# A gated graph network: the reset gate read straight from PSUM, layer 0's product in banks of its own

## What is computed

```python
# layer 0
h = maximum(layernorm(x), 0)
x = x + (adj @ (h @ weight)) + bias
# layer 1: h = maximum(layernorm(x), 0), then five times
m  = adj @ h                       # m_in and m_out are the same product
u3 = h @ u3_w.T + u3_b
z  = sigmoid([m, m] @ w3_w.T + w3_b + u3)
r  = sigmoid([m, m] @ w4_w.T + w4_b + u3)
hv = tanh([m, m] @ w5_w.T + w5_b + (r * h) @ u5_w.T + u5_b)
h  = (1 - z) * h + z * hv
x = x + h
```

## Time and profile before

| | before |
|---|---|
| median of three runs | 1598.83 us (1595.42 to 1601.7) |
| the profiled execution's own time | 1594.64 us |
| its span, first to last instruction | 1592.9 us |
| mean granted clock of TensorE | 0.993 of full speed |
| PE busy | 1553.1 us, 98% |
| DVE, ACT, POOL busy | 67%, 50%, 22% |

### The profile page before, as it was taken

One profiled execution on the slowest core, in us unless ns is written; L12 is line 12 of the kernel. 1 busy time (PEld: TensorE's weight loads), 2 busy tenths in 40 slices (PEclk: granted clock), 3 DMA queues, 4 the chain that ended last, 5 costly groups with the idle time before them and its releaser, 6 DMA issues.

```text
span 1592.9 us, 23652 instructions
## 1 busy us (share of the span) xinstructions
PE 1553.1 (98%) x7471; PEld 721.3 (45%) x7471; DVE 1072.1 (67%) x1982; ACT 793.9 (50%) x1250; POOL 353.5 (22%) x817
## 2 busy tenths in 40 slices
PE   6999999999999999999999999999999999999997
PEld 4444444444444444444444444444444444444443
DVE  7766668666686666866677666676666766686666
ACT  3255544555445554455534555355554555454554
POOL 6230052300603006130062201430024300430000
PEclk8999999999999999999999999999999999999999
DMA  4121113211131111311122111221112211121111
GB/s 149 40 47 33 27 27 83 50 26 37 21 100 28 36 30 40 79 33 32 26 51 74 33 26 31 62 66 26 36 30 56 63 34 32 26 53 47 33 27 53
DMA packets 214238, 71.87 MB, mean 45 GB/s; under 512 B 208192, under 2 KB 209088, under 8 KB 214208
## 3 DMA queue, kind: packets, MB, share of 16 engines
q1 hardware_dynamic: 212480, 70.83, 19.2%
q10 hardware_dynamic: 1728, 0.66, 0.2%
HBM read 13.24 MB, written 8.39 MB: 14 GB/s over the span
## 4 chain that ended last, share of the span: by engine, by line
issue 51%; PE 22%; POOL 18%; DVE 6%; ACT 1%; DMA 1%; POOLq 1%; SPq 1%; DVEq 0%
PE ps_m L561 14%; POOL x_in L457 5%; POOL y L439 3%; POOL x_in L447 2%; POOL newton L330 1%; POOL newton L340 1%; PE ps_v L583 1%; PE ps_u L583 1%; PE ps_v L585 1%; PE ps_u L587 1%; PE ps_u L585 1%; PE ps_v L587 1%; POOL rstd L344 1%; POOL newton L342 1%; DVE m_lo L983 1%
## 5 line engine op out<-in xcount | busy, mean ns | idle before, releaser
L561 PE MATMUL ps_m<-adj_hi,nh_hi 128*128 128x512 f16 x1280 | 485.5, 379 | 2.6 <-ACT nh_hi L740 2.6
L561 PE MATMUL ps_m<-adj_lo,nh_hi 128*128 128x512 f16 x1280 | 485.6, 379 | 0.0
L561 PE MATMUL ps_m<-adj_hi,nh_lo 128*128 128x512 f16 x1280 | 485.6, 379 | 0.0
L764 ACT ACTIVATE m_hi<-ps_m 128x512 f16<-128x512 f32 x192 | 113.2, 589 | 353.8 <-PE ps_m L561 353.8
L983 DVE SCALAR_TENSOR_TENSOR m_lo<-ps_m,m_hi 128x512 f16<-128x512 f32 x192 | 132.0, 688 | 224.8 <-ACT m_hi L764 224.8
L759 ACT ACTIVATE h_hi<-h 128x512 f16<-128x512 f32 x158 | 97.4, 631 | 209.8 <-DVE h L1004 209.8
L311 POOL TENSOR_TENSOR mean<-stats 128x8 f32<-128x8 f32 x23 | 7.4, 322 | 868.8 <-DVE stats L922 868.8
L561 PEld LDWEIGHTS ps_m<-adj_hi,nh_hi 128*128 128x128 f16 x1280 | 125.3, 98 | 152.3 <-issue 3.4
L561 PEld LDWEIGHTS ps_m<-adj_hi,nh_lo 128*128 128x128 f16 x1280 | 125.3, 98 | 151.3 <-issue 0.5
L561 PEld LDWEIGHTS ps_m<-adj_lo,nh_hi 128*128 128x128 f16 x1280 | 125.3, 98 | 149.4 <-issue 0.3
L992 DVE SCALAR_TENSOR_TENSOR cand<-cand,h 128x512 f32<-128x512 f32 x160 | 108.1, 692 | 119.8 <-ACT cand L774 119.8
(11 more groups left out here) (143 smaller groups left out, 2315.3 us busy)
## 6 DMA issues: line engine op xcount, KB each, us to landing
x_in<-in_x_dram SPq DMA_DIRECT2D x16, 512.0 KB, 3.5
...
nh_hi<-h_hi SPq DMA_TRANSPOSE x128, 2.4
nh_lo<-h_lo SPq DMA_TRANSPOSE x128, 2.4
h_hi<-nh_hi SPq DMA_TRANSPOSE x32, 2.4
h_lo<-nh_lo SPq DMA_TRANSPOSE x32, 2.4
n_hi<-h_hi SPq DMA_TRANSPOSE x30, 2.4
```

Source lines behind the costliest of these rows:

```text
L561: last = nc.tensor.matmul(ps_m[half][:, :], a[slot][:, k, :], b[:, k, cols(half)], start=(k == 0 and n == 0), stop=(k == BLOCKS - 1 and n ...
L764: nc.scalar.activation(m_hi[:, cols(half)], ps_m[half][:, :], ACT.Copy, scale=M_SCALE).then_inc(m_hi_done, 1)
```

## The change

WR's product goes on top of h·UZR in ps_u, and ACT's sigmoid for r reads ps_u. After that the product of WZR = WZ - WR goes on top of the same bank, which makes it h·UZR + m·WZ, and z's sigmoid reads it as before. So `hu`, its copy on ACT and the sum on DVE are gone, and so are the banks ps_r. The two banks are now ps_x, and `layer_out` writes there; it is called for each half apart, half 0 after two blocks and half 1 after six (in the very first pass after four). At the start DVE makes the difference WZ - WR with one more operation.

```diff
@@ PE: layer_out takes a half, and writes ps_x
-            def layer_out(p, slot):
+            def layer_out(p, slot, half):
                 g, n = g_layer(p, slot), n_layer(p, slot)
                 if not (is_start(p) and slot == 0):
-                    pe.wait_ge(x1_ready, 2 * n)
...
+                    pe.wait_ge(x1_ready, 2 * n - 1 + half)
@@ PE: layer(0, 1)
-                    layer_out(0, 0)
-                    big_layer(p, slot, 0, range(AHEAD, BLOCKS))
+                    layer_out(0, 0, 0)
+                    big_layer(p, slot, 0, range(AHEAD, HB))
+                    layer_out(0, 0, 1)
+                    big_layer(p, slot, 0, range(HB, BLOCKS))
@@ PE: step
-                    layer_out(*before)
-                    big_step(p, t, slot, 0, range(AHEAD, BLOCKS))
+                    layer_out(*before, 0)
+                    big_step(p, t, slot, 0, range(AHEAD, BLOCKS - AHEAD))
+                    layer_out(*before, 1)
+                    big_step(p, t, slot, 0, range(BLOCKS - AHEAD, BLOCKS))
                 big_step(p, t, slot, 1, range(BLOCKS))
-                if before is not None:
-                    pe.wait_ge(x1_ready, 2 * n_layer(*before) + 2)
-                else:
+                if before is None:
                     pe.wait_ge(z_ready, q)
-                    pe.wait_ge(r_sum, 2 * q)
...
                 for half in range(2):
-                    product(ps_u[half], UZR, h16_hi[slot], h16_lo[slot], half).then_inc(hu_done, 1)
-                    if half == 1:
-                        if before is None:
-                            pe.wait_ge(cand_ready, 2 * q - 1)
-                        product(ps_v[0], WV, m_hi, m_lo, 0, stop=False)
+                    product(ps_u[half], UZR, h16_hi[slot], h16_lo[slot], half, stop=False)
+                for half in range(2):
                     pe.wait_ge(m_hi_done, 2 * g + half + 1)
                     pe.wait_ge(m_lo_done, 2 * g + half + 1)
-                    product(ps_r[half], WR, m_hi, m_lo, half).then_inc(r_done, 1)
-                for half in range(2):
-                    pe.wait_ge(hu_copied, 2 * q + half + 1)
-                    product(ps_u[half], WZ, m_hi, m_lo, half, start=False, reopen=True).then_inc(z_done, 1)
-                    if half == 0:
-                        if before is None:
-                            pe.wait_ge(cand_ready, 2 * q)
-                        product(ps_v[1], WV, m_hi, m_lo, 1, stop=False)
+                    product(ps_u[half], WR, m_hi, m_lo, half, start=False).then_inc(r_done, 1)
+                for half in range(2):
+                    if before is None:
+                        pe.wait_ge(cand_ready, 2 * q - 1 + half)
+                    product(ps_v[half], WV, m_hi, m_lo, half, stop=False)
+                    pe.wait_ge(r_ready, 2 * q + half + 1)
+                    product(ps_u[half], WZR, m_hi, m_lo, half, start=False, reopen=True).then_inc(z_done, 1)
@@ ACT: step
-                if before is None:
-                    act.wait_ge(r_sum, 2 * q)
-                for half in range(2):
-                    copy_hu(q, half)
-                    if is_first(t) and slot == 0:
-                        round_y1_half(p, 1, half)
-                if is_end(t) and not is_final(p):
-                    round_y0(p + 1, slot)
                 for half in range(2):
                     c = cols(half)
-                    act.wait_ge(r_sum, 2 * q + half + 1)
-                    nc.scalar.activation(rh[:, c], rh[:, c], ACT.Sigmoid, bias=bias[:, BR:BR + 1],
+                    act.wait_ge(r_done, 2 * q + half + 1)
+                    nc.scalar.activation(rh[:, c], ps_u[half][:, :], ACT.Sigmoid, bias=bias[:, BR:BR + 1],
                                          scale=w_inv[:, GATES:GATES + 1]).then_inc(r_ready, 1)
+                if is_first(t) and slot == 0:
+                    round_y1(p, 1)
+                if is_end(t) and not is_final(p):
+                    round_y0(p + 1, slot)
@@ DVE: sum_weights, step
                 dve.wait_ge(w_sum, 1)
+                nc.vector.tensor_sub(w_raw[:, WZR, :], w_raw[:, WZR, :], w_raw[:, WR, :]).then_inc(w_sum, 1)
+                dve.wait_ge(w_sum, 2)
...
-                for half in range(2):
-                    c = cols(half)
-                    dve.wait_ge(hu_copied, 2 * q + half + 1)
-                    dve.wait_ge(r_done, 2 * q + half + 1)
-                    nc.vector.tensor_add(rh[:, c], ps_r[half][:, :], hu[:, c]).then_inc(r_sum, 1)
-                    if is_first(t) and slot == 0:
-                        rest_y1_half(p, 1, half)
+                if is_first(t) and slot == 0:
+                    rest_y1(p, 1)
```

More of the change, by code:

```diff
@@ L98, in gnn_kernel @@
         l0_inv = sb("l0_inv", [P, 1])
-        L0, WZ, WR, WV, UZR, UV = range(6)
+        L0, WZR, WR, WV, UZR, UV = range(6)
         GATES, CAND = range(2)
@@ L150, in gnn_kernel @@
         ps_u = [bank("ps_u0"), bank("ps_u1")]
-        ps_r = [bank("ps_r0"), bank("ps_r1")]
-        ps_adj = ps_r + ps_v + ps_u
+        ps_x = [bank("ps_x0"), bank("ps_x1")]
+        ps_adj = ps_x + ps_v + ps_u
         w0_in = sem("w0_in")
@@ L187, in gnn_kernel @@
         end_done = sem("end_done")
-        hu_done = sem("hu_done")
         r_done = sem("r_done")
@@ L489, in scale_weights @@
                 pool.wait_ge(w_op, 5)
-                for w, by, also in ((WZ, GATES, m_inv[:, :]), (WR, GATES, m_inv[:, :]), (WV, CAND, m_inv[:, :]),
+                for w, by, also in ((WZR, GATES, m_inv[:, :]), (WR, GATES, m_inv[:, :]), (WV, CAND, m_inv[:, :]),
                                     (UZR, GATES, 1.0 / SCALE16), (UV, CAND, 1.0 / SCALE16)):
@@ L537, in transpose_weights @@
                 for k in range(1, 6):
-                    last = nc.tensor.transpose(ps_r[k // 5][:, (k - 1) % 4 * D:((k - 1) % 4 + 1) * D],
+                    last = nc.tensor.transpose(ps_u[k // 5][:, (k - 1) % 4 * D:((k - 1) % 4 + 1) * D],
                                                w_raw[:, k, :], ident[:, :])
@@ L594, in transpose_h @@
                 last.then_inc(done, 1)
-            def layer_out(p, slot):
+            def layer_out(p, slot, half):
                 g, n = g_layer(p, slot), n_layer(p, slot)
                 if not (is_start(p) and slot == 0):
-                    pe.wait_ge(x1_ready, 2 * n)
-                for half in range(2):
-                    pe.wait_ge(m_hi_done, 2 * g + half + 1)
-                    pe.wait_ge(m_lo_done, 2 * g + half + 1)
-                    for k in range(HB):
-                        block = slice((half * HB + k) * P, (half * HB + k + 1) * P)
-                        out_block = ps_u[half][:, k * D:(k + 1) * D]
-                        nc.tensor.matmul(out_block, m_hi[:, block], w_hi[:, L0, :], start=True, stop=False)
-                        nc.tensor.matmul(out_block, m_hi[:, block], w_lo[:, L0, :], start=False, stop=False)
-                        last = nc.tensor.matmul(out_block, m_lo[:, block], w_hi[:, L0, :], start=False, stop=True)
-                    last.then_inc(l0_done, 1)
+                    pe.wait_ge(x1_ready, 2 * n - 1 + half)
+                pe.wait_ge(m_hi_done, 2 * g + half + 1)
+                pe.wait_ge(m_lo_done, 2 * g + half + 1)
+                for k in range(HB):
+                    block = slice((half * HB + k) * P, (half * HB + k + 1) * P)
+                    out_block = ps_x[half][:, k * D:(k + 1) * D]
+                    nc.tensor.matmul(out_block, m_hi[:, block], w_hi[:, L0, :], start=True, stop=False)
+                    nc.tensor.matmul(out_block, m_hi[:, block], w_lo[:, L0, :], start=False, stop=False)
+                    last = nc.tensor.matmul(out_block, m_lo[:, block], w_hi[:, L0, :], start=False, stop=True)
+                last.then_inc(l0_done, 1)
             def finish_candidate(q):
@@ L765, in round_m @@
                                      ).then_inc(m_hi_done, 1)
-            def copy_hu(q, half):
-                act.wait_ge(hu_done, 2 * q + half + 1)
-                nc.scalar.activation(hu[:, cols(half)], ps_u[half][:, :], ACT.Copy).then_inc(hu_copied, 1)
             def candidate(q):
@@ L934, in layer_sum @@
                     dve.wait_ge(x_biased, n + 1)
-                    nc.vector.scalar_tensor_tensor(out=flat(x1[slot], half), in0=ps_u[half][:, :],
+                    nc.vector.scalar_tensor_tensor(out=flat(x1[slot], half), in0=ps_x[half][:, :],
                                                    scalar=l0_inv[:, :], in1=flat(x_in[slot], half),
```

19 lines of the change are left out of this document (8 added, 11 removed).

## The result

| | before | after |
|---|---|---|
| median | 1598.82 us (4 runs, 1595.42 to 1601.7) | 1581.31 us (4 runs, 1580.66 to 1581.79) |
| the profiled execution's own time | 1594.64 us | 1581.27 us |
| its span | 1592.9 us | 1579.4 us |

The ratio is 0.9892, with a 95% interval of 0.9877 to 0.9906: faster by 1.1%. The prediction said 1586.7 us, with a range of 1582 to 1594. Between the two profiled executions it is 13.4 us. Two questions follow: where the sum missed 1.3 us, and why the medians differ by 4.1 us more than the profiles. The kernel before was timed beside every experiment too; one such execution, of 4278.55 us, counts as slow and is left out.

The account below looks back on a forecast made before the run. PE, busy 98% of the span, bounds the kernel, so only its waits count. Terms -12.1 + 1.2 + 0 - 1.5 + 0.3 = -12.1 us, from 1598.83 to a median of 1586.7 us, range 1582 to 1594.

Parts of the forecast that it names:

- layer_out's second half: First step of slot 0, pairs 1 to 7: PE's seven waits for m_lo half 1 go, minus 12.1 us.
- Given back: Candidate's product in the next step: rh_lo half 0 late by 0.17 us, seven times, plus 1.2 us.
- The 0.15 us between a producer's end and the matmul: Lead a late producer's end needs before PE's slot, charged for rh_lo and for r's sigmoid.
- The new wait in the products: WZR waits for r's sigmoid, starting T + 2.14 (T: step's first product's start); slack 0.18 us, cost 0.
- each weight load would show in front of such a wait: Rival: weight loads not hidden under matmuls lose 0.10 us at 160 waits, 16 us, giving 1602.7; 3%.
- The end: After the last step's products: r comes sooner, both PE waits go, minus 1.5 us.
- The start: PE's first big product waits for adj_lo, delayed by the added difference on DVE: plus 0.3 us.
- for a median I take 1598.83 - 12.1: Step from profile to median: the summed gain taken off the earlier median of three runs, giving 1586.7 us.
- more is won: Rival: no give-back and a quicker end, 1585 us; forecast and this rival together 77%.
- The forecast of 960 us for DVE: Sign expected in the changed profile: DVE busy for near 960 us.

Follow-up runs that it names:

- e2: The changed kernel with layer_out's two halves in a row again, behind the second block: 1593.12 us.
- e12: The changed kernel with six big matmuls, not twelve, between layer_out's halves: 1584.37 us.
- e4: The kernel before with only layer_out's halves put apart, gates and banks unchanged: 1586.69 us.
- e8: The changed kernel with z's WZ - WR product right behind WR's, ahead of WV's: 1611.77 us in one run.
- e1: The kernel before, unedited, run again in eleven executions: 1597.75 us (1594.96 to 1599.35).
- e5: The kernel before with POOL's addition of the bias rows in eight pieces: 1601.68 us, ratio 1.0000.
- e6: e4's kernel with POOL's addition of the bias rows in eight pieces: 1588.42 us.
- e9: The kernel before with POOL's bias addition for slot 0 of the next pair waiting until rh_lo is written: 1594.33 us, ratio 0.9967.
- e3: e2's kernel with eight unused matmuls of 512 columns between layer_out's halves, keeping TensorE busy in the wait: 1593.19 us.

## Why the prediction was right, and where it was wrong

**layer_out's second half, -12.1: right.** The waits are gone; the pair went from 193.48 to 191.75 us. e2 prices it at 11.8, and e12, with a part of the cover, fits.

**Given back, +1.2: 0 in the changed kernel.** POOL started at 260.83, close to the 260.7 in the prediction, but took 3.48 us where the earlier trace rows have 3.94, so nh_hi came at 263.83 in one piece and rh_lo started at 267.08, not 267.35. Its first half ends at 267.77, and the product needed it by 268.0. The step that failed here is the duration taken over for POOL. Before, one of POOL's eight pieces, beside DVE's nh_lo with two operands in SBUF, took twice its time:

```profile
264.46 0.73 DVE L965 SCALAR_TENSOR_TENSOR nh_lo<-x_in,nh_hi 128x512 f16<-128x512 f32 x1 [0.24 <-ACT nh_hi L740]
...
264.61 0.91 POOL L457 TENSOR_SCALAR x_in<-x,rstd,shift 128x128 f32<-128x128 f32 x1
```

The others took 0.45. In the change both sigmoids of r stand ahead of nh_hi on ACT, nh_lo starts at 264.49 when POOL is done (260.83 + 3.48 = 264.31), and no piece is held. e4, with the old gates, still has the long piece (0.92 at 264.57) and does give 0.30 back in each pair. That this order is the cause is read from the traces; no run tests it alone. The 0.15 us between a producer's end and the matmul doesn't follow from the 269.50 and 269.74 that the prediction gives for it (0.24); it is 252.09 to 252.24 of the earlier trace rows.

**The new wait in the products, 0: right.** The first sigmoid starts at T + 2.14 in all 80 steps and takes 0.77. In the kernel before the second copy of hu didn't start there in all 80, as the prediction said, but in 72; in seven it started at T + 2.37 and in one at T + 3.6. Nothing hung on it. e8 shows that the slack is small and what passing it costs: three matmuls less cost 30.5 us. That each weight load would show in front of such a wait didn't come true either.

**The end, -1.5: right,** 1.47 us: no wait at 1567.54, and the wait for the last h stays as it was (4.5 us).

**The start, +0.3: 0.1.** adj_lo is later (PE waits 0.61 us there, 0.17 before), but nh_hi at 54 us takes up all except 0.18. What follows changed more than the prediction saw: before, TensorE ran at half clock from 54.0 to 57.4 in the profiled execution; after, at full clock, and then waits 1.70 us for m_lo. By the candidate's product the two are level (76.26 and 76.37). What the clock does there is not the change's doing: with the old gates it fell at 54 us in the profiles of before, e1 and e5 and not in e4, e6 and e9. e9, at full clock, reaches that product at 76.17, so the clock hardly moves the sum. By these terms the sum is -12.1 - 1.5 + 0.1 = -13.5, and the profiled executions show -13.4.

**The step that failed for the median** is "for a median I take 1598.83 - 12.1". It took for granted that the other executions of the kernel before spend their 4.2 us in places that the change leaves alone. They spend them in waits of 1.08 us for rh_lo (e1), some four at the median, which an added wait on POOL takes away altogether (e9, 1594.33), and the change takes them away too. The rival "more is won" had the missing give-back right, but its 1585 rests on the same step. DVE and POOL after, in pair 1:

```profile
298.63 3.45 DVE L1087 TENSOR_TENSOR rh_lo<-rh,rh_hi 128x512 f16<-128x512 f32 x2
...
298.96 2.57 POOL L445 TENSOR_TENSOR x_in<-x_in,b_rows 128x1024 f32<-128x1024 f32 x1 [0.18 <-POOL y L437]
```

Here POOL catches the second rh_lo in every pair. But without sum and copy the pair of rh_lo starts 1.07 us sooner in this step (T + 4.62, in e1 T + 5.69), and an rh_lo that is held until 302.1 is still in time, by 0.2 us (its matmul starts at 302.43 without a wait). So the changed kernel pays nothing for it and its executions lie within 1.1 us. e3 shows it within one execution: POOL catches rh_lo in five of its seven pairs and misses it in pairs 3 and 5, and every pair is 193.48 to 193.49 us long. Against e9, the kernel before without these waits, the change is worth 13.0 us, near the 13.5 of its own terms; the other 4.5 of the 17.5 are waits that it covers. The forecast of 960 us for DVE missed by 24, of which the holding makes 15: 160 x (786 - 692) ns, with the 692 of the kernel before; the other 9 are not traced.
